# First attention of a four-stage network: four buffers for the x rows and another order of turns, loads and small operations

## The chip, the cores and the metric

The kernel runs on one core of a Trainium2 chip. The core has TensorE (PE, with its weight loads PEld), VectorE (DVE), ScalarE (ACT), GpSimd (POOL), and SyncE (SP), which here issues nearly all DMAs. The metric is the device time of one execution in microseconds (us). The kernel before took 2070.7 us, the median of 3 runs (2068.66 to 2072.9).

## The reference

The network has four stages: an attention (L0_xattn), a mixture of experts (L0_ffn), a second attention (L1_xattn) and a second mixture (L1_ffn). Only the first stage, its last batch's preparations for the second, and the first loads are touched by the change. Cut to what matters:

```python
# stage 1, four batches b; context ctx is 512x256, x is 512x512 per batch
query = einsum('bnc,dc->bnd', teacher_features, Wq) + bq      # d = 128
key = einsum('bnc,dc->bnd', teacher_features, Wk) + bk
attention = softmax(einsum('bnd,bmd->bnm', query, key), axis=-1)
x_m = einsum('bln,bmn->blm', teacher_logits, attention)       # x rows are normalised first
# stage 3 needs keys and values of the same context: k = _ln(y @ Wk + bk), v = y @ Wv + bv
# stage 2: gate = x @ Wg[e] + x @ Ga[e] @ Gb[e], and so on
```

The kernel computes stage 3's keys (with their norm over heads of 32) and values inside stage 1, because the context is on the core there, and parks them in DRAM.

## The kernel before, in words

Every product in fp32 accuracy is made of three TensorE products of high and low halves (`mm3`, lines 55 to 57); ACT makes the high half (a copy), DVE or POOL the low half (the difference). So every operand goes through ACT and then DVE before TensorE can use it. The five engines run five programs written out by hand, each in strict order; semaphores (`then_inc`, `wait_ge`) join them. No scheduler moves anything.

The first attention (`first_attention`) runs four batches b. For each batch TensorE does, in this order: four key products (`key_or_value`, 0 to 3), transposition of the normalised x rows (`x_turn`, four of them, through line 101), query and key of the next batch (`query_or_key`), transposition of the attention shares (`at_turn`), four value products, the next batch's scores (`scores`), four mixed products (`mixed`: shares times x) with transpositions of the normalised keys between them (`k_turn`).

What the names mean: `CT` is the loaded context, `CYh` and `CYl` its halves (`split_ct_act`, `split_ct_low`); `XNa` the normalised x rows (`normal`, on ACT, two buffers), `XTah` and `XTal` the halves of their transposition; `ATa` the shares, `ATTah` and `ATTal` the halves of their transposition; `KW` the raw keys, `KQ` their squares (`square`), `ksum` and `vv` the variances, `yy` their power -1/2 (POOL, `pow`); `VO` the values on their way to DRAM (two buffers); `KG`, `KH`, `KL` normalised keys and their halves; `qTa`, `kTa` the query and key; `KId` a table of picks that POOL builds in rows of `ATa` and SP stores, so that the first exponentials may only overwrite `ATa` once that store has landed (`st_ki`). `WK`, `WKd`, `WV`, `WVd` are key and value weights; of the first two the means over each head are taken off first (`head_means`, `center`). `stats` and `row_factors` make the norm of the x rows (DVE, then POOL).

In batch 3 there is no next batch; TensorE does low-rank products of the first expert's gate (g) and up (u) weights there (`lora_pe`, line 1209), DVE adds them to the loaded weights `STG` (`lora_dve`, line 1329), ACT and DVE make halves `Wg0h`, `Wg0l`.

A bank of PSUM or a buffer is reused only after its readers are through: `x_turn` n waits for `XTal` n-2 (`freed67`), `normal` k for the transposition k-2, `mixed` 2 for the update of `X` that reads bank 0 (`o_x`).

## Time and profile before

| what | us |
|---|---|
| median of 3 runs | 2070.7 |
| the profiled execution, whole | 2068.12 |
| its span, first to last instruction | 2066.3 |
| TensorE busy in the span | 1994.7 (97%) |
| stage 1 until its last transposition of keys ends | 207.15 |
| TensorE busy in those | 169.82 |
| TensorE waits in them, before the first product | 10.5 |

The profile is of one execution. An engine's time is split into instructions, and the idle time before one is put down to the instruction or DMA that released it. TensorE is near full from stage 2 on; the idle time lies in the first tenth. "PEclk" or "clock" is the TensorE clock that was granted: 1.00 is 2.4 GHz and a stretch at 1.2 GHz counts half. A product of 512 columns starts 0.23 us after the one ahead at the full clock and 0.43 us after it at the low one; as it lasts 0.39 us at the full clock, a stop also costs the overlap of some 0.2 us.

### The profile page before, as it was taken

What the parts mean: (1) busy time and instruction counts of PE and PEld (TensorE: products, weight loads), DVE (VectorE), ACT (ScalarE), POOL (GpSimd) and SP (SyncE); (2) the same over time, 40 slices, a digit from 0 to 9 for tenths busy, and PEclk for the clock granted to TensorE, in tenths of its full rate; (3) what the DMA queues carried; (4) which work ended last, traced back from release to release, by engine and by line L of the source; (5) the groups of instructions that cost most, each with busy time, mean ns of one, the idle gap of its engine ahead of it and who ended that gap; (6) DMA issues with size and microseconds to landing.
All of it is one profiled execution on the core that took longest, in us unless ns stands there. A gap on an engine that the chain in (4) does not pass through costs nothing. (4 is left out here: it accounts for less than half of the span.)

```text
span 2066.3 us, 29550 instructions
## 1 busy us (share of the span) xinstructions
PE 1994.7 (97%) x11805; PEld 1585.1 (77%) x11805; DVE 945.7 (46%) x1555; ACT 767.6 (37%) x1210; POOL 675.9 (33%) x629
## 2 busy tenths in 40 slices
PE   6888999999999999999999999999999999999997
PEld 4776687788888888888888888756666667889996
DVE  6775433222222222221221245687677664656664
ACT  5464611212212121121211222356565655247664
POOL 5444301011101111011111127446464323226674
PEclk9998999999999999999999999999999999999999
DMA  5232200103012030010100001734343330169994
GB/s 196 77 128 90 74 1 26 41 1 123 21 63 81 1 122 21 21 41 1 41 21 19 28 1 44 179 73 102 84 103 88 73 118 32 42 226 269 264 270 112
DMA packets 91336, 171.32 MB, mean 83 GB/s; under 512 B 10864, under 2 KB 35952, under 8 KB 88240
## 3 DMA queue, kind: packets, MB, share of 16 engines
q1 hardware_dynamic: 80896, 148.96, 23.5%
q0 software_dynamic: 10304, 20.47, 4.5%
q8 instruction: 94, 1.54, 0.3%
q14 instruction: 42, 0.34, 0.1%
HBM read 131.51 MB, written 54.13 MB: 90 GB/s over the span
## 5 line engine op out<-in xcount | busy, mean ns | idle before, releaser
L1570 POOL TENSOR_TENSOR ML<-MT,MH 128x512 fp32r<-128x512 f32 x128 | 164.9, 1292 | 791.2 <-ACT MH L1372 791.0
L1514 DVE SCALAR_TENSOR_TENSOR X<-PS,WT,X 128x512 f32<-128x512 f32 x128 | 96.0, 750 | 391.1 <-PE PS L57 390.6
L1372 ACT ACTIVATE MH<-MT 128x512 fp32r<-128x512 f32 x128 | 80.9, 632 | 512.1 <-DVE MT L1441 512.1
L55 PE MATMUL PS<-HH,Wg0h 128*128 128x512 f32 x512 | 200.6, 392 | 0.2 <-issue 0.2
L55 PE MATMUL PS<-Wd0h,MH 128*128 128x512 f32 x512 | 199.6, 390 | 0.1
L56 PE MATMUL PS<-HL,Wg0h 128*128 128x512 f32 x512 | 199.7, 390 | 0.0
L57 PE MATMUL PS<-HH,Wg0l 128*128 128x512 f32 x512 | 199.6, 390 | 0.0
L55 PE MATMUL PS<-HH,Wu0h 128*128 128x512 f32 x512 | 199.5, 390 | 0.0
L56 PE MATMUL PS<-HL,Wu0h 128*128 128x512 f32 x512 | 199.3, 389 | 0.0
L57 PE MATMUL PS<-HH,Wu0l 128*128 128x512 f32 x512 | 199.2, 389 | 0.0
L56 PE MATMUL PS<-Wd0l,MH 128*128 128x512 f32 x512 | 199.2, 389 | 0.0
L57 PE MATMUL PS<-Wd0h,ML 128*128 128x512 f32 x512 | 199.2, 389 | 0.0
L1441 DVE TENSOR_TENSOR MT<-PS,SG 128x512 f32<-128x512 f32 x128 | 88.4, 690 | 232.2 <-POOL ML L1570 159.8
L1979 ACT ACTIVATE PTB<-PS 128x512 f32<-128x512 f32 x256 | 138.7, 595 | 111.4 <-PE PS L1904 110.5
L2063 DVE TENSOR_REDUCE VB<-PS 128x2 f32<-128x992 f32 x232 | 148.9, 684 | 41.7 <-PE PS L1889 41.4
L1343 ACT ACTIVATE SG<-PS 128x512 f32<-128x512 f32 x128 | 76.4, 597 | 224.4 <-PE PS L57 224.4
L55 PEld LDWEIGHTS PS<-HH,Wg0h 128*128 128x128 f32 x512 | 96.4, 188 | 21.9 <-issue 2.1
L55 PEld LDWEIGHTS PS<-HH,Wu0h 128*128 128x128 f32 x512 | 96.1, 188 | 21.7 <-issue 1.5
L55 PEld LDWEIGHTS PS<-Wd0h,MH 128*128 128x128 f32 x512 | 96.1, 188 | 21.4 <-issue 1.3
L57 PEld LDWEIGHTS PS<-HH,Wg0l 128*128 128x128 f32 x512 | 96.4, 188 | 20.3
L56 PEld LDWEIGHTS PS<-HL,Wg0h 128*128 128x128 f32 x512 | 96.4, 188 | 19.8
L57 PEld LDWEIGHTS PS<-Wd0h,ML 128*128 128x128 f32 x512 | 96.1, 188 | 20.1
(481 smaller groups left out, 4300.6 us busy)
## 6 DMA issues: line engine op xcount, KB each, us to landing
RAW<-Wd SPq DMA_DIRECT2D x23, 1536.0 KB
HH<-Kd SPq DMA_DIRECT2D x48, 256.0 KB, 4.1
HL<-Qd SPq DMA_DIRECT2D x48, 256.0 KB, 6.3
STG<-in_Wg SPq DMA_DIRECT2D x8, 1024.0 KB, 5.2
STG<-in_Wu SPq DMA_DIRECT2D x8, 1024.0 KB, 5.2
STG<-in_Wd SPq DMA_DIRECT2D x8, 1024.0 KB, 5.3
X<-in_x SPq DMA_DIRECT2D x16, 256.0 KB, 8.5
Vd<-VO SPq DMA_DIRECT2D x16, 256.0 KB, 2.0
```

The source lines that it names most:

```text
L55: e.matmul(out_, a_[0], b_[0], start=start, stop=False)
L56: e.matmul(out_, a_[0], b_[1], start=False, stop=False)
L57: return e.matmul(out_, a_[1], b_[0], start=False, stop=stop)
L1343: e.activation(SG[:, f, :], PS[:, bank["g", i], :], ACT.Silu).then_inc(g_silu, 1)
L1372: e.activation(M[0][:, f, :], MT[i % 2][:, :], ACT.Copy).then_inc(m_h, 1)
L1441: e.tensor_tensor(MT[i % 2][:, :], PS[:, bank["u", i], :], SG[:, f, :], ALU.mult).then_inc(u_mul, 1)
L1514: e.scalar_tensor_tensor(X[:, k, :], PS[:, bank["d", 4 * n + q], :], WT[:, k, x:x + 1], X[:, k, :], ALU.mult, ALU.add).then_inc(d_x, 1)
L1570: e.tensor_tensor(M[1][:, f, :], MT[i % 2][:, :], M[0][:, f, :].bitcast(f32), ALU.subtract).then_inc(m_l, 1)
L1979: e.activation(PT[u % 2][:, 2 * pr:2 * pr + 2, :], PS[:, p % 2, :].rearrange("p (h q) -> p h q", h=2), ACT.Exp, scale=SCALE).then_inc(t_ex ...
L2063: e.tensor_reduce(MX[s % 2][:, q:q + 2, h, t], PS[:, SBANK:SBANK + 2, lo:hi], axis=X_, op=ALU.max).then_inc(s_max, 1)
```

## The change

Eight things change, all in the first attention (and in what it does ahead for stage 2):

1. The x rows get four buffers: the two `VO` buffers join `XN`. All four `normal` of batches 1 to 3 are done at the end of the batch before; in batch 0 the last two come later. `value` waits for the transposition of the row that lay in its `VO`.
2. TensorE's order: x rows 0 and 1, then query and key of the next batch together, then x rows 2 and 3; the first value product stands ahead of the first transposition of shares. Query and key wait for the first piece of `CYl` only. ACT and DVE follow that order; `square` 3 and `variance` 1 move behind x row 1.
3. DVE does values 0 and 1 earlier (before and after the first two `ATTal`), and the next batch's first maxima and exponentials after the second `ATTal`.
4. The variance is finished, and the power taken, for 16 heads at a time, four times a batch, rather than once for 64.
5. SP loads the context first, then the query and key weights; `g` and `temp` follow later.
6. In `picks_pool` the selects work on two columns and are then copied out to 512.
7. At the start the low half of `WKd` moves from POOL to DVE, the order of centring changes.
8. In batch 3 the low-rank products and their sums go in halves, with the low half of the gate weight behind the norm of the keys.

```diff
     def picks_pool(e, rows):
-        e.memset(rows, 1.0).then_inc(made_ki, 1)
+        e.memset(rows[:, :, 0:512:511], 1.0).then_inc(made_ki, 1)
...
+        for lo, hi, at in ((1, 496, 0), (496, 511, 511)):
+            e.tensor_copy(rows[:, :, lo:hi], rows[:, :, at:at + 1].to_broadcast([16, 4, hi - lo])).then_inc(made_ki, 1)
...
+        XN += VO
...
         def sp(e):
-            e.dma_start(bqk[:, 0:2], a["bqk0"]).then_inc(ld_qk, 16)
+            load_ct(e, 0)
...
         def query_or_key(e, b, j):
-            e.wait_ge(ct_l, 3 * b + 3)
+            e.wait_ge(ct_l, 3 * b + 1)
...
             if b == 0 and v == 0 and n == 0:
-                e.wait_ge(k_sub, 3)
+                e.wait_ge(k_sub, 2)
...
-                for j in range(2):
-                    x_turn(e, b, 2 * j)
-                    x_turn(e, b, 2 * j + 1)
-                    if more:
-                        query_or_key(e, b + 1, j)
+                x_turn(e, b, 0)
+                x_turn(e, b, 1)
+                if more:
+                    query_or_key(e, b + 1, 0)
+                    query_or_key(e, b + 1, 1)
+                else:
+                    two_front["lora_pe"](e, "g", 0)
+                x_turn(e, b, 2)
+                x_turn(e, b, 3)
                 if b == 3:
-                    two_front["lora_pe"](e, "g", 0)
                     two_front["lora_pe"](e, "g", 1)
                 for j in range(4):
+                    key_or_value(e, b, 4 + j)
                     if j % 2 == 0:
                         at_turn(e, b, j)
                         at_turn(e, b, j + 1)
-                    key_or_value(e, b, 4 + j)
...
         def normal(e, k):
-            if k >= 2:
-                e.wait_ge(xt_mm, k - 1)
-            e.activation(XN[k % 2][:, :], X[:, k, :], ACT.Identity, bias=nmr[:, k:k + 1],
+            if k >= 4:
+                e.wait_ge(xt_mm, k - 3)
+                if k % 4 >= 2:
+                    e.wait_ge(st_v[k % 2], 32 * (k // 4))
+            e.activation(XN[k % 4][:, :], X[:, k, :], ACT.Identity, bias=nmr[:, k:k + 1],
...
+                    if more and n == 1:
+                        query_or_key_high(e, b + 1, 0)
+                        query_or_key_high(e, b + 1, 1)
+                    if n == 1:
+                        square(e, b, 3)
+                    if b == 0 and n == 1:
+                        normal(e, 2)
+                        normal(e, 3)
+                        shares(e, 0, 0)
+                        shares(e, 0, 1)
...
-                    normal(e, 4 * b + 4)
-                    normal(e, 4 * b + 5)
+                    for k in range(4 * b + 4, 4 * b + 8):
+                        normal(e, k)
...
+            at = slice(16 * n, 16 * n + 16)
+            e.tensor_reduce(ksum[:, at], heads(KQ[n % 2][:, :]), axis=X_, op=ALU.add).then_inc(k_var, 1)
+            e.wait_ge(k_var, 2 * i + 1)
+            e.tensor_scalar(vv[:, at], ksum[:, at], 1.0 / 32, 1e-6, ALU.mult, ALU.add).then_inc(k_var, 1)
...
-            center(e, chain, slice(0, 2))
+            query_or_key_low(e, 0, 0)
+            center(e, chain, slice(0, 1))
+            query_or_key_low(e, 0, 1)
+            big_low(e, 0, k_sub)
             maxima(e, 0, 0)
-            big_low(e, 0, k_sub)
+            center(e, chain, slice(1, 2))
             e.wait_ge(ld_bias, 64)
             head_means(e, chain, slice(2, 4))
             center(e, chain, slice(2, 4))
+            big_low(e, 1, big_l)
...
+                    if b == 3 and n % 2:
+                        two_front["add"](e, "g", n // 2)
...
                 if b == 3:
-                    two_front["low"](e, "g")
-                    two_front["add"](e, "u")
-                e.wait_ge(k_pow, b + 1)
+                    two_front["add"](e, "u", 1)
+                e.wait_ge(k_pow, 4 * b + 4)
...
+                if b == 3:
+                    two_front["low"](e, "g")
...
-                e.wait_ge(k_var, 5 * b + 5)
-                e.tensor_tensor(yy[:, :], vv[:, :], mhalf[:, :], ALU.pow).then_inc(k_pow, 1)
+                for n in range(4):
+                    at = slice(16 * n, 16 * n + 16)
+                    e.wait_ge(k_var, 2 * (4 * b + n) + 2)
+                    e.tensor_tensor(yy[:, at], vv[:, at], mhalf[:, at], ALU.pow).then_inc(k_pow, 1)
...
+        def lora_half(e, n, half):
+            for c in (2 * half, 2 * half + 1):
+                lora_sum(e, 4 * n + c)
```

TensorE in batch 1, as a difference: rows of the next batch's query (`wqT`) and key (`wkT`), of x transposed from `XNa` or `VO`, of shares `ATa` and of values (`WV1`).

```order
 L57 MATMUL PS<-CY0h,wqTl 128x512
-L101 MATMUL PS<-ident,XNa 128x128 x8
 L55 MATMUL PS<-CY0h,wkTh 128x512
 L56 MATMUL PS<-CY0l,wkTh 128x512
@@ -207,5 +206,5 @@
 L56 MATMUL PS<-CY0l,wkTh 128x512
 L57 MATMUL PS<-CY0h,wkTl 128x512
-L101 MATMUL PS<-ident,ATa 128x128 x8
+L101 MATMUL PS<-ident,VO 128x128 x8
 L55 MATMUL PS<-WV1h,CY1h 128x512
 L56 MATMUL PS<-WV1l,CY1h 128x512
```

The second pair of x transpositions moved from between query and key to behind them, and now reads the two `VO`.

ACT in batch 0, behind the first two normalised x rows, before:

```order
L428 ACTIVATE KQ0<-KW 128x512
L428 ACTIVATE KQ1<-KW 128x512
L490 ACTIVATE XTah<-PS 128x4x128
L421 ACTIVATE XNa0<-X,nmr,rstd0 128x512
L490 ACTIVATE XTah<-PS 128x4x128
L421 ACTIVATE XNa1<-X,nmr,rstd0 128x512
L401 ACTIVATE qTah<-PS,bqk 128x512
L490 ACTIVATE XTah<-PS 128x4x128 x2
L401 ACTIVATE kTah<-PS,bqk 128x512
```

The same place on ACT now:

```order
L443 ACTIVATE KQ0<-KW 128x512
L504 ACTIVATE XTah<-PS 128x4x128 x2
L414 ACTIVATE qTah<-PS,bqk 128x512
L414 ACTIVATE kTah<-PS,bqk 128x512
L443 ACTIVATE KQ1<-KW 128x512
L436 ACTIVATE VO0<-X,nmr,rstd0 128x512
L436 ACTIVATE VO1<-X,nmr,rstd0 128x512
L448 ACTIVATE ATa0<-ATa0,sma 128x512 x4
L504 ACTIVATE XTah<-PS 128x4x128 x2
```

The last two normalised rows (now in `VO`) moved behind the high halves of query and key, and the four shares (`ATa`, which stood ahead of the first normalised row) stand behind them.

DVE in batch 3, from the last row means to the update of `X`, before:

```order
L1433 BN_AGGR mv<-st 128x2 x4
L1321 TENSOR_TENSOR Wg0l<-STG00,Wg0h 128x2048
L1329 TENSOR_TENSOR STG01<-PS,STG01 128x512 x4
L674 TENSOR_TENSOR tt_<-yy 128x64
L676 TENSOR_TENSOR tt_<-tt_,vv 128x64
L678 TENSOR_SCALAR tt_<-tt_ 128x64
L680 TENSOR_TENSOR yy<-yy,tt_ 128x64
L683 TENSOR_TENSOR KW<-KW,yy 128x512 x4
L692 SCALAR_TENSOR_TENSOR X<-PS,TG,X 128x512 x2
```

The same place on DVE now:

```order
L1473 BN_AGGR mv<-st 128x2 x4
L1365 TENSOR_TENSOR STG01<-PS,STG01 128x512 x2
L704 TENSOR_TENSOR tt_<-yy 128x64
L706 TENSOR_TENSOR tt_<-tt_,vv 128x64
L708 TENSOR_SCALAR tt_<-tt_ 128x64
L710 TENSOR_TENSOR yy<-yy,tt_ 128x64
L713 TENSOR_TENSOR KW<-KW,yy 128x512 x4
L1357 TENSOR_TENSOR Wg0l<-STG00,Wg0h 128x2048
L727 SCALAR_TENSOR_TENSOR X<-PS,TG,X 128x512 x2
```

The low half `Wg0l` moved from ahead of the sums of the up weight to between the norm of the keys and the update of `X`.

## Rows read from the trace of the kernel before

**Rows 1.** The page: the span and TensorE's busy time, share and instructions.
```profile
span 2066.3 us, 29550 instructions
...
PE 1994.7 (97%) x11805; PEld 1585.1 (77%) x11805; DVE 945.7 (46%) x1555; ACT 767.6 (37%) x1210; POOL 675.9 (33%) x629
```
**Rows 2.** Stretches: length; busy PE, PEld, DVE, ACT, POOL; TensorE clock; DMA share, GB/s.
```profile
0.00:37.01 37.01, 16.61 (x55) 12.46 (x55) 26.67 (x53) 17.73 (x32) 15.67 (x29) 0.93 0.70 252
37.01:77.26 40.25, 38.65 (x181) 31.62 (x182) 25.10 (x53) 23.94 (x46) 24.61 (x18) 0.94 0.26 93
77.26:119.77 42.51, 37.84 (x181) 30.77 (x180) 30.91 (x69) 23.84 (x46) 19.34 (x20) 0.96 0.15 56
119.77:161.47 41.70, 36.90 (x181) 29.50 (x180) 31.32 (x66) 22.53 (x43) 21.67 (x22) 1.00 0.42 140
161.47:207.15 45.68, 39.82 (x144) 26.43 (x143) 27.36 (x48) 16.67 (x26) 15.95 (x9) 0.81 0.26 92
```
**Rows 3.** What TensorE waited for, 0 to 207.1: total, times, longest, in us.
```profile
PE PS L101 <- DVE XTal L646: 9.0, 6, 2.7
PE PS L55 <- DVE WK1l L555: 3.3, 1, 3.3
PE PS L55 <- DVE VO L603: 3.3, 4, 0.9
PE PS L1209 <- DVE STG L1329: 2.4, 1, 2.4
PE PS L55 <- DVE X L692: 2.2, 3, 0.9
```
**Rows 4.** Instructions in order of time, batch 0: start, length, and idle before.
```profile
3.18 0.94 SPq L231 DMA_DIRECT2D CTa<-in_ctxT  x2
...
20.65 0.69 ACT L415 ACTIVATE ATa<-PS,mxa 128x512 f32<-128x512 f32 x1 [1.35 <-DMA KId<-ATa]
...
29.67 2.46 DVE L547 BATCH_NORM_STATS2 st<-X 128x6 f32<-128x512 f32 x4
...
33.70 2.55 ACT L433 ACTIVATE ATa<-ATa,sma 128x512 f32<-128x512 f32 x4
...
35.37 0.24 POOL L718 TENSOR_SCALAR nmr<-nmr 128x4 f32<-128x4 f32 x1
...
37.01 1.97 PE L101 MATMUL PS<-ident,XNa 128*128 128x128 f32 x8 [4.98 <-ACT XNa L421]
```
**Rows 5.** The same in batch 1, in the order the prediction uses them.
```profile
73.58 1.51 ACT L421 ACTIVATE XNa<-X,nmr,rstd 128x512 f32<-128x512 f32 x2
...
78.99 0.63 ACT L428 ACTIVATE KQ<-KW 128x512 f32<-128x512 f32 x1 [1.51 <-DVE ksum L596]
...
82.14 0.63 PE L101 MATMUL PS<-ident,XNa 128*128 128x128 f32 x4 [2.46 <-DVE XTal L646]
...
101.54 2.50 DVE L683 TENSOR_TENSOR KW<-KW,yy 128x512 f32<-128x512 f32 x4
```
**Rows 6.** The same in batch 2: DVE's low context, and POOL beside it.
```profile
118.19 2.71 DVE L527 TENSOR_TENSOR CY1l<-CTa,CY1h 128x1024 fp32r<-128x1024 f32 x3 [1.61 <-ACT CY1h L395]
```
**Rows 7.** The same in batch 3: low-rank products, and the gate weight's low half.
```profile
167.21 7.33 PE L1209 MATMUL PS<-LB,LA 64*128 64x512 f32 x8
...
190.55 2.26 DVE L1321 TENSOR_TENSOR Wg0l<-STG,Wg0h 128x2048 fp32r<-128x2048 f32 x1
...
193.56 1.95 PE L1209 MATMUL PS<-LB,LA 64*128 64x512 f32 x4 [2.40 <-DVE STG L1329]
```
**Rows 8.** Small DVE operations beside POOL ones, at the start and in stage 3.
```profile
23.13 2.37 POOL L555 TENSOR_TENSOR WKd1l<-KW,WKd1h 128x1024 fp32r<-128x1024 f32 x1 [12.37 <-ACT WKd1h L455]
...
23.28 2.25 DVE L567 TENSOR_SCALAR means<-means 128x32 f32<-128x32 f32 x1
...
1240.11 2.90 POOL L1002 TENSOR_TENSOR yy<-vv,mhalf 128x16 f32<-128x16 f32 x1
...
1242.27 0.17 DVE L982 TENSOR_SCALAR gs<-gs 128x16 f32<-128x16 f32 x1
```

More of the change, by code:

```diff
@@ L370, in pe @@
                         at_turn(e, b, j + 1)
-                    key_or_value(e, b, 4 + j)
-                    if more and j % 2:
+                    elif more:
                         scores(e, b + 1, j // 2)
@@ L483, in act @@
                     split_ct_act(e, b + 1)
-                for n in range(0 if b else 2, 4):
+                for n in range(0 if b else 2, 3):
                     square(e, b, n)
@@ L501, in act @@
                     e.activation(ATT[0][:, c, :], PS[:, 6 + c % 2, :], ACT.Copy).then_inc(at_h, 1)
-                if more:
-                    exponentials(e, b + 1, 0)
-                    exponentials(e, b + 1, 1)
-                    shares(e, b + 1, 0)
+                    if more and c == 1:
+                        exponentials(e, b + 1, 0)
                 if b == 3:
@@ L509, in act @@
                     two_front["high"](e, "u")
+                if more:
+                    exponentials(e, b + 1, 1)
                 keys_high(e, b, 0)
                 if more:
+                    shares(e, b + 1, 0)
                     shares(e, b + 1, 1)
@@ L629, in dve @@
                 stats(e, 0, k)
+            temperature(e)
             for n in range(4):
@@ L642, in dve @@
                 key(e, 4 * b + 3)
-                variance(e, 4 * b + 1)
                 for n in range(4):
@@ L647, in dve @@
                                     XT[0][:, :, n * P:(n + 1) * P].bitcast(f32), ALU.subtract).then_inc(xt_l, 1)
-                    if more and n % 2:
-                        query_or_key_low(e, b + 1, n // 2)
+                    if n == 1:
+                        variance(e, 4 * b + 1)
+                    if more and n == 1:
+                        query_or_key_low(e, b + 1, 0)
+                        query_or_key_low(e, b + 1, 1)
+                    if b == 3 and n % 2:
+                        two_front["add"](e, "g", n // 2)
                 variance(e, 4 * b + 2)
                 variance(e, 4 * b + 3)
-                e.wait_ge(k_var, 5 * b + 4)
-                e.tensor_scalar(vv[:, :], ksum[:, :], 1.0 / 32, 1e-6, ALU.mult, ALU.add).then_inc(k_var, 1)
-                if b == 3:
-                    two_front["add"](e, "g")
                 for c in range(4):
+                    if c % 2 == 0:
+                        value(e, 4 * b + c)
+                    if b == 3 and c == 2:
+                        two_front["add"](e, "u", 0)
                     e.wait_ge(at_h, 4 * b + c + 1)
@@ L660, in dve @@
                     if c % 2:
-                        value(e, 4 * b + c // 2)
-                        if c == 3 and more:
+                        value(e, 4 * b + c)
+                        if c == 1 and more:
                             maxima(e, b + 1, 0)
@@ L665, in dve @@
                             row_stats(e, b - 1, (0, 1))
-                value(e, 4 * b + 2)
-                value(e, 4 * b + 3)
                 if b:
@@ L684, in dve @@
                                     ALU.mult).then_inc(k_norm, 1)
-                if more:
-                    maxima(e, b + 1, 1)
+                if b == 3:
+                    two_front["low"](e, "g")
                 for n in range(4):
                     k = 4 * b + n
-                    if more:
-                        recip(e, k + 4)
+                    if more and n == 0:
+                        maxima(e, b + 1, 1)
+                        for m in range(2):
+                            recip(e, 4 * b + 4 + m)
+                    if more and n == 2:
+                        for m in range(2, 4):
+                            recip(e, 4 * b + 4 + m)
                     e.wait_ge(o_mm, k + 1)
@@ L1552, in first_mixture @@
             lora_pe=lambda e, which, half: lora_pe(e, 0, which, (half,)), high=lambda e, which: weight_h(e, 0, which),
-            add=lambda e, which: lora_dve(e, 0, which), low=lambda e, which: weight_l(e, 0, which),
+            add=lambda e, which, half: lora_half(e, nth(0, which), half), low=lambda e, which: weight_l(e, 0, which),
             row=row, router_high=router_high, stat=row_stat, mean=row_mean, factors=factors)
```

58 lines of the change are left out of this document (27 added, 31 removed).

## The prediction

> **What bounds the kernel now.** The page comes first: TensorE is busy for 97% of the span [rows 1]. Then the table of stretches, cut at each batch's first transposition of x [rows 2]: TensorE works 16.6, 38.7, 37.8, 36.9 and 39.8 us in 207.15 us, so 37.3 us of the whole kernel's idle 72 lie here. No other engine is full (DVE 141 us of 207), so the stage is bound by chains between engines, not by an engine. The clock column tells a second loss: a mean of 0.81 over the last 45.68 us means that 2 x 0.19 x 45.68 = 17 us went by at 1.2 GHz, in which half of the work is lost; batches 1 and 2 have 0.96 and 1.00. The list of waits names the chains [rows 3]: 9.0 us for the low half of transposed x (XTal, a long and a short one in each of batches 1 to 3, so 3.0 a batch), 3.3 for the first key weight, 3.3 for a value leaving its bank (0.8 a batch), 2.4 for the low-rank sums, 2.2 for the update of X (0.7 in each of batches 0 to 2); the first normalised x row adds 4.98 [rows 4]. From stage 2 on TensorE has hardly a gap, so I carry what stage 1 gains to the end one for one.
>
> I go by batch, each from its first x transposition. Where no row has a length, an operation of 512 columns counts 0.6 to 0.7 us on DVE or ACT (four statistics took 2.46, a square 0.63) [rows 4, 5].
>
> **Start and batch 0: about -0.5.** The context was issued at 3.18 [rows 4], behind five transfers; now it is first. The weights of query and key come behind it and are needed too, so the first product gains between 0 and 2.4 us; I take 1.5. Statistics of x begin at 29.67 on DVE [rows 4]. Ahead of them DVE loses a stall of 2.05 (a scale of 32 columns took 2.25 beside POOL's WKd1l, which goes) [rows 8] and gets that WKd1l itself, 1.13 by half of a 2048-column difference [rows 7]. So they begin at 29.67 - 1.5 - 2.05 + 1.13 = 27.25. POOL's factors were through at 35.61, 5.94 later, but the normalised row waited for four shares until 36.15 and reached TensorE at 37.01 [rows 4]. The shares now stand behind, so TensorE starts at 27.25 + 5.94 + 0.86 = 34.05: 3.0 us of head start. The wait for WK1l (3.3) lies ahead of this point and is no further gain; the five or so microseconds that the keys gain there end in a longer wait for x. The first exponentials waited for the picks' store until 20.65 [rows 4]; as many bytes stand ahead of it as before, so small selects are worth 0 there (a microsecond either way at most).
>
> Then batch 0 gives it back. Rows 2 and 3 of x are normalised only behind both high halves of query and key and a square: 0.69 + 0.63 + 0.75 on ACT after TensorE's last key product, a wait of 2.1. Behind them on ACT stand the fourth row, four shares (2.55) and XTah, then XTal on DVE: 4.6 us against 2.5 of TensorE work, a wait of 1.9 before the shares are transposed. Every stop also costs the overlap of two products, 0.2. That is 4.4, against one stop of 1.0 for a value before: +3.4. The stop for X before the third mixed product (0.9) goes, since DVE has done its maxima by then. Sum -3.0 + 3.4 - 0.9 = -0.5. Ends: -4 if the new waits were hidden, +3 if no head start came.
>
> **Batch 1: -3.1.** Before: 3.0 for XTal (its long wait is the 2.46 at 82.14) [rows 5], 0.8 for a value, 0.7 for X [rows 3], four overlaps, and some 0.8 lost to the low clock (0.04 x 2 x 42.5 = 3.4 us low, half of it idle) [rows 2]: 6.1. After: ACT does four normalisations where it did two (1.51), so the context's halves come 1.5 later, and CYl ends about 1.0 after TensorE's first x transposition. Behind it on DVE stand key 2, variance 0 and its scale, then ACT's third square, which waits for that variance already (1.51 at 78.99) [rows 5], then XTah and XTal: five steps of 0.6, so XTal is there 4.1 after. TensorE now has two transpositions and both query and key (0.8 + 2.9) before it asks: a wait of 0.4, then 0.2. New: XTah 2 stands behind two high halves and a square, so the transposition of shares waits 0.8 and 0.15. The value's wait goes: values 0 and 1 leave earlier, and what value now waits for, a row's transposition, is long over. X comes later against TensorE: from the last value product DVE has that value, the row statistics (2.8), the Newton step (1.0), the norm (2.50) [rows 5], maxima and X, 9.4 us against 7.9 of scores, two mixed products and two transpositions: 1.5. Sum after 3.05. The power is never late: its first pieces run while DVE is elsewhere. Ends: -6 and 0.
>
> **Batch 2: -0.9.** Before: the same 3.0, 0.8, 0.7 and overlaps, no low clock [rows 2, 3]: 5.3. After: as batch 1, but the low context took 2.71 here [rows 6], since its small pieces stood beside POOL's KL; later by 1.5, it meets that work again, 1.4 more: 4.4. Ends: -4 and +1.
>
> **Batch 3: -6.9.** Before: 3.0 for XTal, 0.8 for a value, 2.40 for the sums [rows 3, 7] and overlaps, 6.9; the low clock: eight passes of low-rank products took 7.33 at 0.92 each, where four took 1.95 later, 0.49 each: 3.4 lost [rows 7]; the transpositions and first value products around them lose 2.6 by the same ratio, and the rest of the 17 us low I put at 1.7. Together 14.6. After: TensorE has a low-rank half (2.0) between the x transpositions, which hides most of XTal: 0.2 and 0.2; the second half waits 0.9 for the sums, which are now behind XTal and a variance. The u products no longer wait. But the gate's low half (2.26) [rows 7] now stands between the norm and X: 1.45 before the key transpositions and 2.0 behind them. 4.75 in waits. From the first transposition to the first value there are then some 7 us with transpositions, low-rank passes and waits only, which before went low; I let the clock fall for one stretch, 2.3, and give 0.6 for the chance of another at the X wait. 7.7. Difference -6.9; ends -11 (no low clock, X hidden) and 0.
>
> The Trainium skill speaks against this part ("TensorE: Matmul & The Clock Gate", section "PE-mode transpose"): transpositions do not count as TensorE being busy for the clock. This case's rows agree as far as the low-rank passes of 167.21 and what stands round them stayed at 1.2 GHz. By that rule the 2.3 stays; without it batch 3 would give -9.2.
>
> **Powers in quarters.** DVE gets four scales of 16 heads a batch for one of 64, 0.5 us more, beside POOL's powers. A scale of 32 columns was held to the end of a POOL difference (23.13 + 2.37 = 25.50; 23.28 + 2.25 = 25.53), but one of 16 beside a power of 2.90 took 0.17 [rows 8]. So 0.5 in all over the batches' slack: 0. The Trainium skill ("SBUF — State Buffer", section "SBUF: two separate sides") has the ports that VectorE and GpSimd share as an exclusive lock, held for a whole instruction by who comes first. The first pair of rows agrees, the second does not; by the rule the time is that of the port rival.
>
> **Sum.** -0.5 - 3.1 - 0.9 - 6.9 = -11.4 on the profiled execution's 2068.1 (span 2066.3 and 1.8 around it) is 2056.7. That execution lies 2.6 below the median of 2070.7, so I forecast 2059, with 2053 to 2065 for this case alone.
>
> **Rivals.**
> - *The new waits are hidden.* TensorE's waits of 4.4, 3.05, 4.4 and 4.75 vanish too, because ACT and DVE run ahead further than I count. For: neither is over 76% busy in any stretch [rows 2]. Against: each wait is a count of operations in strict order. 2059 - 16.6 = 2042. Chance 0.14.
> - *The four normalisations hold up batches 1 and 2.* The context's halves, 1.5 later, push key 2, the squares and XTal by more than TensorE's extra 1.45 of key products covers, and X's wait grows: the 4.0 of these batches is lost. For: DVE is busy 31 of 42 us there and strictly ordered. 2063. Chance 0.15.
> - *The port.* Each scale behind a running power waits for its end, up to 2.9; the third and fourth of a batch come close enough to lose some 2.3 on DVE, half of which reaches TensorE: 4 x 1.2, so 2064. Against: the row of 0.17. Chance 0.08.
> - *The clock turns it round.* What happened round the low-rank products of batch 3 happens in all four batches, since x transpositions, waits and share transpositions now stand nearer together: 6.0 lost in each (3.4 + 2.6), of which 2.3 is already counted. 2059 + 4 x 6.0 - 2.3 = 2081; with two batches low so the gain is all but gone, from the third it is slower. For: three of the four batches went low before. Against: batch 2 had its long wait and kept 1.00 [rows 2]. Chance 0.06.
>
> The forecast keeps 0.57. Faster by over 0.2% is under 2066.6 (about what can be told from no change): nearly all of the forecast, the first rival, most of the second and third, 0.82. Within 0.2%: 0.12, from the upper ends of the second and third. Slower: 0.06, the clock. The range for 8 in 10 runs from 2046, in the first rival, to 2067, above the second and third.
>
> **What would show it.** The first product near 9.0; the first x transposition near 34, then two waits near 2 in batch 0 on a normalised row in VO and on XTal; in batches 1 and 2 XTal waits under 1.5 and X waits of 1.5; no wait for VO or the low-rank u sums; in batch 3 X late behind Wg0l, and a clock over 0.9. I am wrong if the first value of a batch starts later against its first x transposition than before, if a scale of 16 takes over 1 us, or if stage 2 takes up a gap that stage 1 gave.

## The result, and the profile after

The changed kernel took 2058.25 us (median of 5 runs, 2050.63 to 2061.13) against 2072.90 for the kernel before in the same comparison: a ratio of 0.9925, with a 95% interval from 0.990 to 0.995. Faster was right, and 2059 was forecast. The profiled execution took 2061.13 us, the longest of the five, as before's (2068.12) was shorter than all five of its runs; so the sum is tested on the stretches of the traces rather than on these two totals.

The page after: span, TensorE, and the granted clock by fortieths of the span.

```profile
span 2059.1 us, 29588 instructions
...
PE 1993.1 (97%) x11805; PEld 1586.0 (77%) x11805; DVE 946.1 (46%) x1568; ACT 767.6 (37%) x1210; POOL 672.1 (33%) x642
...
PEclk9998999999999999999999999999999999999998
```

The same stretches as in [rows 2], cut at the first transposition of x of each batch (last transposition of keys, first product with the low-rank rows of Wd as the last two cuts; columns as there):

```profile
0.00:33.62 33.62, 17.07 (x55) 12.45 (x55) 23.18 (x54) 14.87 (x28) 9.25 (x30) 0.95 0.77 277
33.62:75.64 42.02, 39.44 (x181) 32.11 (x181) 26.24 (x55) 27.36 (x51) 26.01 (x21) 0.92 0.25 89
75.64:114.77 39.13, 36.58 (x181) 29.47 (x180) 30.73 (x70) 23.45 (x46) 20.94 (x24) 1.00 0.16 61
114.77:154.99 40.22, 36.59 (x181) 29.47 (x180) 32.86 (x72) 23.10 (x45) 22.67 (x25) 1.00 0.41 145
154.99:191.47 36.48, 33.18 (x140) 22.83 (x139) 27.56 (x50) 14.74 (x23) 17.42 (x15) 0.95 0.35 113
191.47:213.63 22.16, 18.09 (x86) 14.35 (x84) 9.53 (x17) 16.34 (x27) 9.55 (x11) 0.77 0.33 112
```

TensorE's waits up to 215 us, which answer to [rows 3] (total, times, longest):

```profile
PE PS L55 <- DVE X L727: 4.6, 3, 1.9
PE PS L101 <- ACT QY L1396: 3.9, 2, 3.6
PE PS L101 <- DVE XTal L674: 3.8, 5, 1.5
PE PS L101 <- ACT XNa L436: 3.2, 1, 3.2
PE PS L101 <- ACT VO L436: 2.1, 1, 2.1
PE PS L101 <- DVE KW L713: 1.3, 1, 1.3
PE PS L1245 <- DVE STG L1365: 0.2, 1, 0.2
```

XTal fell from 9.0 to 3.8, the values' 3.3 are gone, the low-rank sums' 2.4 became 0.2; X grew from 2.2 to 4.6, and VO, KW and a long QY are new. The kernels by stretch, in us (batch 3 to its last transposition of keys, "front" from there to the first low-rank product of Wd):

| kernel | ratio to before | x starts | b 0 | b 1 | b 2 | b 3 | front | sum |
|---|---|---|---|---|---|---|---|---|
| before | 1 | 37.01 | 40.25 | 42.51 | 41.70 | 45.24 | 19.43 | 226.14 |
| changed | 0.9925 | 33.62 | 42.02 | 39.13 | 40.22 | 36.48 | 22.16 | 213.63 |
| e1 low early | 0.9900 | 34.52 | 41.76 | 39.15 | 40.24 | 32.81 | 18.30 | 206.78 |
| e2 batch 3 undone | 0.9960 | 33.85 | 42.06 | 39.11 | 40.24 | 43.65 | 18.28 | 217.19 |
| e3 batch 0 rows early | 0.9913 | 33.23 | 38.71 | 39.14 | 40.27 | 36.48 | 21.86 | 209.69 |
| e4 power whole | 0.9937 | 33.76 | 45.14 | 39.56 | 40.71 | 34.87 | 21.44 | 215.48 |
| e5 three edits | 0.9889 | 33.52 | 38.71 | 39.26 | 40.21 | 32.00 | 19.54 | 203.24 |
| e6 variance back | 0.9929 | 33.34 | 41.44 | 38.61 | 39.73 | 36.45 | 22.20 | 211.77 |
| e7 query, key apart | 0.9937 | 33.26 | 41.50 | 39.38 | 40.48 | 36.33 | 21.72 | 212.67 |
| e8 old loads | one run | 33.91 | 42.86 | 39.11 | 40.24 | 34.91 | 22.51 | 213.54 |
| e9 old selects | one run | 34.36 | 41.81 | 40.13 | 40.25 | 36.33 | 19.21 | 212.09 |
| e10 square back | 0.9950 | 33.46 | 41.09 | 41.82 | 40.81 | 37.47 | 21.70 | 216.35 |
| e11 two buffers | 0.9915 | 33.74 | 41.78 | 38.54 | 39.54 | 37.08 | 20.01 | 210.69 |
| e12 e5, context first | 0.9878 | 34.12 | 38.70 | 37.99 | 38.79 | 31.99 | 20.04 | 201.63 |

Each ratio is to runs of the kernel before in the same comparison (medians 2071.29 to 2073.83); each row of stretches is from one profile.

The changed kernel leads by 12.5 at the end of this table. What is left of the span took between 1839.8 and 1845.9 in all fourteen profiles (1840.2 before, 1845.5 after), with no pattern in the edits: that spread makes the two profiled totals only 7 apart. The medians are 14.7 apart, so the lead is not lost behind the table. A part of the spread is the clock: in the 130 us that begin 1510 us behind the end of the table it was 0.99 in five profiles (before, e5, e8, e9, e12; the rest took 1839.8 to 1844.0) and 0.97 in the other nine (1842.9 to 1845.9).

The rows also tell what a stretch is worth as a measure. In the kernels whose edits leave a stretch alone, batch 2 repeats to 0.06, and batch 1 to 0.15 but for e9. Batch 3 and the front do not: in the kernels that leave it alone, batch 3 took 36.33 to 36.48 (changed, e3, e7, e9) or 34.91 (e8), and the front, wherever Wg0l is late (see e1 below), 19.21 to 22.51.

### The profile page after: what moved, and what is told of

Its sections match the earlier page's. It is cut to its first block and busy times, and to the rows that moved or that the text cites. A ratio compares the mean times of both kernels' runs of the same rounds, so it can differ in the third digit from the quotient of the medians.

```text
span 2059.1 us, 29588 instructions
## 1 busy us (share of the span) xinstructions
PE 1993.1 (97%) x11805; PEld 1586.0 (77%) x11805; DVE 946.1 (46%) x1568; ACT 767.6 (37%) x1210; POOL 672.1 (33%) x642
## 5 line engine op out<-in xcount | busy, mean ns | idle before, releaser
L57 PEld LDWEIGHTS PS<-HH,Wu0l 128*128 128x128 f32 x512 | 96.1, 188 | 20.1
```

What stands on the lines that cost most here:

```text
L57: return e.matmul(out_, a_[1], b_[0], start=False, stop=stop)
```

## The experiments

**Where batch 3's stops and the front's come from.** In the changed kernel VectorE makes Wg0l at 180.78, between the norm of the keys and X.

```diff
                         value(e, 4 * b + c)
+                        if b == 3 and c == 1:
+                            two_front["low"](e, "g")
...
-                if b == 3:
-                    two_front["low"](e, "g")
                 for n in range(4):
                     k = 4 * b + n
```

> The changed kernel with one edit: in batch 3 the low half of the gate weight (Wg0l) is made on VectorE right behind the second value, in a gap of 2.1 us, rather than between the norm of the keys and X. Theory A: the place of Wg0l is what made batch 3 stop for X (1.86), and, since its end releases the 1 MB load of the next weight just ahead of the stores of the key halves, also what made these stores late (4.3 to 4.9 us instead of 2.1 to 2.5) and so the stop of 3.60 for row QY that stage 2's front shows. Then the X stop goes, the QY stop falls to 2.2 or less, and of the low clock behind them some goes too: about 5 us less than the changed kernel (2053, between -3 and -8). Rival B: the QY stop is ACT's and POOL's own chain of key halves, too late for a faster TensorE wherever the load stands; then only the X stop goes, the QY stop stays at 3 or grows, and the time falls by 2 or less.

Measured: 2052.90 (ratio 0.990, 0.9885 to 0.9915). First the changed kernel's rows on SP, ACT and PE (start, length, idle before):

```profile
183.09 0.39 SPq L1194 DMA_DIRECT2D STG<-in_Wd  x1
183.53 0.50 SPq L287 DMA_DIRECT2D Kd<-KH  x1
...
183.87 0.47 PE L55 MATMUL PS<-ATTah,XTah 128*128 128x512 f32 x1 [1.86 <-DVE X L727]
...
192.94 0.63 ACT L463 ACTIVATE KH<-KG 128x512 fp32r<-128x512 f32 x1 [2.95 <-DMA Kd<-KL]
...
196.54 1.09 PE L101 MATMUL PS<-ident,QY 128*128 128x128 f32 x4 [3.60 <-ACT QY L1396]
```

(`KH`, `KL` go to DRAM as `Kd`; `QY` is a normalised row of x for stage 2.) Then e1's, on SP and PE:

```profile
175.07 0.59 SPq L1194 DMA_DIRECT2D STG<-in_Wd  x1
184.10 0.33 SPq L287 DMA_DIRECT2D Kd<-KH  x1
...
181.58 1.09 PE L101 MATMUL PS<-ident,KW 128*128 128x128 f32 x8 [1.26 <-DVE KW L715]
...
192.19 0.63 PE L101 MATMUL PS<-ident,QY 128*128 128x128 f32 x4 [2.24 <-ACT QY L1396]
```

And e1's batch 3 and front as stretches (length, PE busy, clock, DMA share, GB/s):

```profile
155.67:188.48 32.81, 31.36 (x139) 1.00 0.36 127
188.48:206.78 18.30, 14.40 (x85) 1.00 0.39 132
```

The weight load is issued 0.4 us ahead of the key stores in the one and 9 us ahead in the other. The first two of these stores, with the time from issue to landing at the end of a line, in the changed kernel and under it in e1:

```profile
Kd<-KH SPq DMA_DIRECT2D x1, 256.0 KB, 6.6
Kd<-KL SPq DMA_DIRECT2D x1, 256.0 KB, 8.1
```

```profile
Kd<-KH SPq DMA_DIRECT2D x1, 256.0 KB, 3.1
Kd<-KL SPq DMA_DIRECT2D x1, 256.0 KB, 2.3
```

So the stores right behind the load were later than e1's expectation has it: its 4.3 and 4.9 are medians of four stores, of which two stood behind the load. In the changed kernel ScalarE waits 2.95 for such a store before it may write KH again, and row QY stands behind that. In the nine kernels with Wg0l late, ScalarE waited 1.03 to 4.57 for that store, and the QY stop was 2.24 (twice) to 5.18; in the five with Wg0l early (e1, e5, e12) or in its old place (before, e2) ScalarE never waited, and the stop was 2.24. Theory A is shown for the stops. Its sizes, 3.7 us in batch 3 and 3.9 in the front, hold a part that comes and goes with the clock. In e4 and e8 the stop for X is 1.86 too, but batch 3's clock is 1.00; e4's row:

```profile
159.17:194.04 34.87, 31.57 (x140) 1.00 0.32 104
```

So 2.1 of the 3.7 (34.9 against 32.81) go with the stop itself, the rest with the clock. In the front, the median is 21.72 in the nine kernels with Wg0l late and 19.43 in the other five: some 2.3 is what repeats.

**Batch 3's part undone.** TensorE's side is below; VectorE sums g behind the last variance again, and Wg0l and the sums of u stand behind the row statistics.

```diff
-                else:
-                    two_front["lora_pe"](e, "g", 0)
                 x_turn(e, b, 2)
                 x_turn(e, b, 3)
                 if b == 3:
+                    two_front["lora_pe"](e, "g", 0)
                     two_front["lora_pe"](e, "g", 1)
...
```

> The changed kernel with the eighth part undone: in batch 3 both halves of the low-rank gate products stand behind the fourth transposition of x, their sums behind the last variance, Wg0l and the sums of u behind the row statistics, and the gate weight is loaded ahead of the low-rank rows. Theory A (the prediction's): batch 3's gain is this part's, so batch 3, from its first x transposition to its last transposition of keys, goes from 36.5 back to about 43.4 (45.2 in the kernel before), with a low clock in the low-rank passes again, and stage 2's front stops for QY as before (2.2). Together +5 to +7: about 2064. Rival B: batch 3 gains because four normalised rows are ready at its start, whatever the low-rank order; then batch 3 stays under 39 and the time within 2 of the changed kernel.

Measured: 2065.09 (0.996, 0.9947 to 0.9974), batch 3 43.65. Theory A, to 0.3 in batch 3; the front is 18.28, with the QY stop at 2.24. TensorE's stops there:

```profile
157.34 1.25 PE L101 MATMUL PS<-ident,VO 128*128 128x128 f32 x8 [1.04 <-DVE XTal L673]
163.34 2.48 PE L1243 MATMUL PS<-LB,LA 64*128 64x512 f32 x4 [2.84 <-DVE STG L1363]
184.15 2.80 PE L1243 MATMUL PS<-LB,LA 64*128 64x512 f32 x4 [3.59 <-DVE STG L1363]
```

Its batch 3 and front as stretches:

```profile
155.26:198.91 43.65, 36.18 (x140) 0.88 0.28 95
198.91:217.19 18.28, 14.39 (x86) 1.00 0.39 132
```

7.5 of stops against 3.3 in the changed kernel, and a clock of 0.88 against 0.95: 10.5 us low against 3.6, half of it lost. 4.2 of stops and 3.4 of clock make up the 7.2 that this part is worth (the two overlap a little).

**Batch 0.** ScalarE's order there:

```diff
-            normal(e, 0)
-            normal(e, 1)
+            for k in range(4):
+                normal(e, k)
...
+                    if b == 0 and n == 1:
+                        shares(e, 0, 0)
+                        shares(e, 0, 1)
                     if more and n == 1:
                         query_or_key_high(e, b + 1, 0)
                         query_or_key_high(e, b + 1, 1)
...
```

> The changed kernel with another order on ScalarE in batch 0 alone: all four normalised rows before the first XTah, and the four shares ahead of the high halves of query and key. Theory A: the stops of 2.15 for the third row (in VO) and of 0.39 for XTal in batch 0, and the low clock right behind them, are nothing but that order; they go, nothing takes their place since TensorE has two transpositions and twelve query and key products meanwhile, and batch 0 goes from 42.0 to about 38.5: 2055. Rival B: the stop moves, to XTal (XTah then comes 1.5 later) or to the first scores (query and key later by 2.6): batch 0 stays over 41, and the time is that of the changed kernel within 1.

Measured: 2056.65 (0.9913, 0.990 to 0.9927). TensorE in batch 0, the changed kernel first, then e3:

```profile
41.56 1.94 PE L101 MATMUL PS<-ident,VO 128*128 128x128 f32 x8 [2.15 <-ACT VO L436]
...
45.92 1.23 PE L101 MATMUL PS<-ident,ATa 128*128 128x128 f32 x8 [0.39 <-DVE XTal L674]
```

```profile
38.78 1.03 PE L101 MATMUL PS<-ident,VO 128*128 128x128 f32 x8
...
42.26 1.22 PE L101 MATMUL PS<-ident,ATa 128*128 128x128 f32 x8 [1.06 <-DVE XTal L672]
```

Batch 0 is 38.71 as expected, though not quite by theory A: the stop for VO goes, that for XTal comes to 1.06. In the changed kernel the low clock behind the first stop (a transposition of 1.94 for 1.03) hid it; in e1, where that transposition took 1.33 behind the same stop of 2.15, it was 1.65. So of the 3.3 a part is the clock (0.92 over batch 0 in the changed kernel, 0.96 in e3 and e1): against e1, with a clock as in e3, the order is worth 3.0. The gain of 3.3 in the trace is 1.6 in the medians, inside their spread.

**Powers.**

```diff
-                for n in range(4):
-                    at = slice(16 * n, 16 * n + 16)
-                    e.wait_ge(k_var, 2 * (4 * b + n) + 2)
-                    e.tensor_tensor(yy[:, at], vv[:, at], mhalf[:, at], ALU.pow).then_inc(k_pow, 1)
+                e.wait_ge(k_var, 8 * b + 8)
+                e.tensor_tensor(yy[:, :], vv[:, :], mhalf[:, :], ALU.pow).then_inc(k_pow, 1)
...
```

> The changed kernel with the fourth part half undone: POOL takes the power of all 64 heads in one instruction per batch, behind the fourth variance, as the kernel before did; VectorE still finishes the variance in four pieces. Theory A (the prediction's): worth 0, since VectorE asks for the powers well behind; the Newton step of batch 3 still finds them, 3 us to spare. Within 1 us of the changed kernel. Rival B (the port): powers in pieces hold up VectorE's scales; then the whole power is faster by 3 or more. Rival C: the pieces are what made the norm early enough; then a wait for the power shows ahead of the Newton step and costs 2 or more.

Measured: 2060.67 (0.9937, 0.9922 to 0.9953). e4's batch 0, on POOL, DVE and PE:

```profile
49.01 10.59 POOL L762 TENSOR_TENSOR yy<-vv,mhalf 128x64 f32<-128x64 f32 x1 [8.37 <-DVE vv L620]
...
59.63 0.23 DVE L704 TENSOR_TENSOR tt_<-yy 128x64 f32<-128x64 f32 x1 [3.06 <-POOL yy L762]
...
63.19 1.09 PE L101 MATMUL PS<-ident,KW 128*128 128x128 f32 x8 [0.55 <-DVE KW L713]
65.63 0.47 PE L55 MATMUL PS<-ATTah,XTah 128*128 128x512 f32 x1 [1.35 <-DVE X L727]
```

Theory A falls, C holds in batches 0 to 2: one power of 10.6 comes 3.06 late, and TensorE stops 0.55 for KW in each, in batch 0 also for X: 3.1, 0.4 and 0.5 longer, with a clock of 0.90 in batch 0. The port falls too: in the changed kernel, a scale of 16 beside a running power took 0.18 (below).

**All three gains together.** Beside the edits of e1 and e3, the Newton step and half of the norm go ahead of the last sums of u:

```diff
-                if b == 3:
-                    two_front["add"](e, "u", 1)
                 e.wait_ge(k_pow, 4 * b + 4)
...
                 for n in range(4):
+                    if b == 3 and n == 2:
+                        two_front["add"](e, "u", 1)
                     e.tensor_tensor(heads(KW[:, n, :]), heads(KW[:, n, :]), over(yy[:, 16 * n:16 * n + 16], 32),
```

> The changed kernel with three edits: Wg0l early, as in the first experiment; batch 0's four normalised rows and shares early, as in the third; and in batch 3 the Newton step and the norm of the first two keys ahead of the last two sums of u. Theory A: each edit takes away its own stop, and the gains add: 7.7 from batch 3 on by the first trace, 3.3 in batch 0 by the third, and the stop of 1.26 for KW at the first transposition of keys in batch 3 falls under 0.3. By the traces 12, by the medians of the two runs 5.4 and 1.6 and another 1: between 2046 and 2051, I take 2049. Rival B: they share one thing (a stretch at the low clock, or stage 2's front, which starts at a fixed time), so the sum is that of the larger alone: 2053.

Measured: 2048.36 (0.9889, 0.9872 to 0.9905). The gains add in the stretches that the edits touch: batch 0 as in e3, batch 3 0.8 under e1; the KW stop is 0.46, not under 0.3. The front, at 0.91 of the clock, is 1.2 longer than in e1.

**What shortened batches 1 and 2.** Four edits, one at a time.

In e6 VectorE's variance 1 goes back ahead of XTal, from behind the second one:

```diff
                 key(e, 4 * b + 3)
+                variance(e, 4 * b + 1)
                 for n in range(4):
...
-                    if n == 1:
-                        variance(e, 4 * b + 1)
```

> The changed kernel with one edit on VectorE: the variance of key 1 goes back ahead of XTal, where the kernel before had it; TensorE's order, the buffers and ScalarE's order stay. Theory A: XTal was late because VectorE waited in that variance for ScalarE's square; with it there again XTal comes about 1 us later, and TensorE stops for XTal before the third x row 0.9 to 1.5 longer in batches 1 and 2 (0.41 and 1.49 now), and less in 3: +2 to +3, so 2061. Rival B: query and key of the next batch, now together between the x rows, cover it: no stop over 0.6 more in any batch, and the time within 1 of the changed kernel.

Measured: 2057.31 (0.9929). Theory B: the stop before the third row grew by 0.3 in both batches, and that of 0.76 before the shares went. A half microsecond a batch better, not worse.

In e7 key goes behind x rows 2 and 3 in batches 1 and 2, on TensorE as shown, and likewise on ACT and DVE:

```diff
                     query_or_key(e, b + 1, 0)
-                    query_or_key(e, b + 1, 1)
+                    if b == 0:
+                        query_or_key(e, b + 1, 1)
...
+                if more and b:
+                    query_or_key(e, b + 1, 1)
...
```

> The changed kernel with query and key apart again in batches 1 and 2: query behind x rows 0 and 1, key behind rows 2 and 3, on all three engines; the four buffers, variance 1 behind XTal and the early values stay. Theory A: half of the cover for XTal is gone, so TensorE stops 1.45 longer before the third x row (1.9 and 2.9 in batches 1 and 2), and the 0.76 before the transposition of shares goes, since XTal has key's time there: +0.7 a batch, and +1.4 in all: 2060. Rival B: this is where the gain of these batches comes from, so both lose their 3.4 and 1.5: 2063. Rival C: the order is worth nothing, only buffers and variance are: within 0.5.

Measured: 2057.98 (0.9937). The stops are 1.76 and 2.86 as theory A had them, the one before the shares gone, but each batch is only 0.25 longer: nearest to C.

In e10, beside e6's edit, square 3 goes back ahead of XTah on ACT, from behind the second one:

```diff
-                for n in range(0 if b else 2, 3):
+                for n in range(0 if b else 2, 4):
                     square(e, b, n)
...
-                    if n == 1:
-                        square(e, b, 3)
```

> The changed kernel with square 3 on ScalarE back ahead of the first XTah, and so variance 1 on VectorE back ahead of XTal (which alone cost 0.3 a stop and gained 0.76 elsewhere). Theory A: the long stop for XTal before was this chain, square 3 waiting for variance 1 with all of XTah behind it: XTal then comes some 1.5 to 2 later, TensorE stops 1.5 longer before the third x row in batches 1 and 2 and shows a stop in batch 3, in sum +3 to +4: 2061. Rival B: XTal waits for the context's halves and for key 2 on VectorE in any case, so the stop grows by 0.5 or less and the time stays within 1 of the changed kernel.

Measured: 2062.04 (0.995, 0.9931 to 0.9968): theory A for the stops. ScalarE and TensorE in e10's batch 1, and the stop of batch 2:

```profile
77.79 0.63 ACT L443 ACTIVATE KQ<-KW 128x512 f32<-128x512 f32 x1 [1.51 <-DVE ksum L616]
79.19 0.63 ACT L443 ACTIVATE KQ<-KW 128x512 f32<-128x512 f32 x1 [0.76 <-DVE ksum L616]
79.72 1.06 ACT L504 ACTIVATE XTah<-PS 128x512 fp32r<-128x512 f32 x2
...
81.08 1.96 PE L101 MATMUL PS<-ident,VO 128*128 128x128 f32 x8 [1.91 <-DVE XTal L673]
...
123.05 1.26 PE L101 MATMUL PS<-ident,VO 128*128 128x128 f32 x8 [2.88 <-DVE XTal L673]
```

Two squares, each waiting for a variance on VectorE, stand ahead of XTah; batches 1 to 3 are 2.7, 0.6 and 1.0 longer. Of the 2.7 not all is the edit's. The clock has a part (0.96 over the batch, the transposition of 1.96). And in e9, whose edit lies at the start alone, batch 1 is 1.0 longer too: in both, ScalarE had waited for a key half's store at the end of batch 0, which it does not in the changed kernel. e10, then e9:

```profile
68.79 0.63 ACT L463 ACTIVATE KH<-KG 128x512 fp32r<-128x512 f32 x1 [1.04 <-DMA Kd<-KL]
```

```profile
70.46 0.63 ACT L460 ACTIVATE KH<-KG 128x512 fp32r<-128x512 f32 x1 [1.08 <-DMA Kd<-KL]
```

That leaves 1.7 for the edit and the clock in batch 1, and 0.6 in batch 2.

In e11 two buffers serve from batch 1 on, and the last two rows stand behind the first and second XTah:

```diff
-                    for k in range(4 * b + 4, 4 * b + 8):
+                    for k in range(4 * b + 4, 4 * b + 6):
                         normal(e, k)
...
+                    if b and n < 2:
+                        normal(e, 4 * b + n + 2)
...
```

> The changed kernel with only two buffers for the x rows from batch 1 on: the last two rows of a batch are normalised behind the first and second XTah, as before, the values wait for no transposition, and all orders else stay. Theory A: the four buffers by themselves are worth little, since ScalarE gives back at the end of a batch (1.51, so the context's halves come 1.5 earlier) what it pays behind XTah: within 1.5 of the changed kernel, the stop for XTal before the third row near 0 and a stop for the row itself, or for XTal before the shares, of 0.8 to 1.5 in its place. Rival B: the four buffers carry batches 1 and 2, and without them 3.4 and 1.5 are lost: 2063.

Measured: 2056.17 (0.9915, 0.9894 to 0.9937). Theory A: batches 1 and 2 are 0.6 and 0.7 shorter with two buffers, batch 3 0.6 longer. The four buffers carry none of the gain of batches 1 to 3.

**The head start.** e8 has g, biases and weights of query and key ahead of the context on SP again; e9 has POOL's wide fills and selects again, without the copies:

```diff
         def sp(e):
+            consts_sp(e)
+            e.dma_start(bqk[:, 0:2], a["bqk0"]).then_inc(ld_qk, 16)
-            load_ct(e, 0)
             for j, name in enumerate(("wqT0", "wkT0")):
...
+            load_ct(e, 0)
             load_big(e, 0)
```

> The changed kernel with the first six loads in the order of the kernel before (g, query and key biases and weights, then the context); the small selects and the rest stay. Read from the trace alone, by the start of the first product (8.97 in the changed kernel, 10.54 before) and of the first x transposition (33.62). Theory A (the prediction's): the context ahead of the weights is what brought the first product 1.5 earlier, so it comes at 10.5 again, and x about 1 to 1.5 later. Rival B: it was the selects, which no longer slow down VectorE's first differences (2.08 beside a select before, 0.43 now); then the first product stays under 9.5.

```diff
-        e.memset(rows[:, :, 0:512:511], 1.0).then_inc(made_ki, 1)
+        e.memset(rows, 1.0).then_inc(made_ki, 1)
...
-        for lo, hi, at in ((1, 496, 0), (496, 511, 511)):
-            e.tensor_copy(rows[:, :, lo:hi], rows[:, :, at:at + 1].to_broadcast([16, 4, hi - lo])).then_inc(made_ki, 1)
```

> The changed kernel with the sixth part undone: POOL fills and selects all 512 columns of the picks again; the context stays first. Read from the trace, by the first product (8.97 in the changed kernel, 9.34 with the old order of loads, 10.54 before). After the run with the old loads, theory A: the selects held up VectorE's first differences (2.08 beside one before, 0.43 and 0.45 with the small ones), and they are worth most of the 1.57: the first product comes at 10.0 or later, and the first exponentials, which wait for the picks' store, at 20 or later (19.27). Rival B (the prediction's): the small selects are worth 0, the first product stays under 9.5.

One profile each (2057.50 and 2057.78 us): the first product came at 9.34 in e8, at 10.10 in e9. In the other profiles with the changed start it came between 8.73 and 9.36, so e8's cannot be told from them: the order of loads is worth some 0.4, if anything. e9's POOL and VectorE, and under it the changed kernel's VectorE:

```profile
4.63 5.44 POOL L143 TENSOR_SCALAR_AFFINE_SELECT ATa<-ATa 16x1984 f32<-16x1984 f32 x4
...
6.70 2.08 DVE L632 TENSOR_TENSOR wkTl<-XNa,wkTh 128x256 fp32r<-128x256 f32 x1
```

```profile
6.69 0.43 DVE L635 TENSOR_TENSOR wkTl<-XNa,wkTh 128x256 fp32r<-128x256 f32 x1
```

The wide selects hold up a small difference by 1.65, and with it the context's low half: the selects gave the first product 1.1 of its 1.57. x itself came at 33.91 in e8 and 34.36 in e9, the first exponentials at 20.01 and 20.29; in e1, whose start is that of the changed kernel, they came at 34.52 and 21.09. So what the selects give the first product is not shown to reach x.

**One step more.** On e5, the next context's high halves go ahead of x rows 2 and 3:

```diff
                 if b in (1, 2):
                     split_ct_act(e, b + 1)
+                if b:
+                    normal(e, 4 * b + 2)
+                    normal(e, 4 * b + 3)
...
-                    for k in range(4 * b + 4, 4 * b + 8):
+                    for k in range(4 * b + 4, 4 * b + 6):
                         normal(e, k)
```

> The best kernel so far (three edits, 2048.4) with one more: at the turn of batches, ScalarE makes the high halves of the next context before rows 2 and 3 of x rather than behind them. Theory A: the context's low half, on VectorE, is 1.5 late because ScalarE does four rows first (VectorE waits 2.6 for the halves), and key 2, the variance and XTal stand behind it; with the halves earlier the stops for XTal of 0.53 and 1.50 in batches 1 and 2 go, and nothing comes for the rows, which TensorE asks for 4 us later: -1.5 to -2.5, about 2046.5. Rival B: XTal is held by ScalarE's third square and not by the context, so the stops stay: within 0.7 of 2048.4.

Measured: 2047.53 (0.9878, 0.986 to 0.9895). Both stops for XTal before the third row are gone, and batches 1 and 2 are 1.3 and 1.4 shorter than in e5: theory A in the trace. The medians differ by 0.8 only, which their spread does not tell from 0.

## Why the prediction was right, and where it was not

By its own steps, predicted and measured, each against before:

| step | predicted | measured |
|---|---|---|
| start (first x transposition) | -3.0 | -3.4 |
| batch 0 from there | +2.5 | +1.8 |
| batch 1 | -3.1 | -3.4 |
| batch 2 | -0.9 | -1.5 |
| batch 3 | -6.9 | -8.8 |
| stage 2's front | 0 | +2.7 |
| sum | -11.4 | -12.5 |

The sum is nearer than its terms, which is in part luck: batch 3 gave 1.9 more than forecast and four other steps 2.0 more between them, and the front, which the sum had at 0, took 2.7 back. That the median came within 1 of 2059 says less still, as the kernel before ran at 2072.9 this time instead of 2070.7.

**Start.** Right in sum: x at 33.62, forecast 34.05. The statistics began at 26.70 (forecast 27.25), and the scale of 32 columns took 0.18 where it had 2.25, as counted. One term had the wrong cause: 1.5 was put on the context's place among the loads and 0 on the selects; for the first product e8 and e9 show it the other way round.

**Batch 0.** The new waits came where they were put: 2.15 for the third row (2.1), and 0.39 for XTal (1.9) because the clock had fallen to 1.2 GHz behind the first; at the higher clock of e1 it is 1.65. The first is ScalarE's order alone: e3 takes it away; XTal's stays there at 1.06. One of the prediction's own signs of being wrong came here: the first value starts 9.53 after the batch's first x transposition, against 8.03 before. In the other batches it comes earlier (5.21 against 10.23 in batch 1).

**Batches 1 and 2.** The stops came at 0.41, 0.76 and 1.35 in batch 1 (forecast 0.4 and 0.2, 0.8, 1.5), and 1.49 for the first in batch 2. The mechanism was half told. I gave the gain to the covering order of TensorE and the early values; by e10 up to 2.3 of the 4.9 in both, a part of it clock, are the square and the variance that no longer stand ahead of XTah, by e7 TensorE's order is worth 0.25 a batch, and by e11 the four buffers nothing. What the early values give was not undone by itself: the value's stops of 0.79 and 0.80 are gone, and the stops for X grew from 0.87 and 0.57 to 1.35. That the context comes late behind four normalisations was right, as e12 shows.

**Batch 3.** The stops were 0.19, 1.25 and 1.86 (forecast 0.2 and 0.2, 0.9, 1.45, 2.0). The mis-sized term is the clock: before, 0.19 x 2 x 45.24 = 17.2 us were low, half of it lost (8.6); after, 0.05 x 2 x 36.48 = 3.6, so 1.8 lost. That is 6.8 gained where 7.7 less 2.9 was counted. It did not fall at the transpositions and low-rank passes either (1.00 from 155 to 175), but behind the stop for X. In e1 passes and transpositions stand as they did, the X stop is gone, and the clock is 1.00 throughout. The stop alone does not settle it, though: in e4 and e8 it is 1.86 as well, and the clock of batch 3 is 1.00. The rule of the Trainium skill on transpositions ("TensorE: Matmul & The Clock Gate", section "PE-mode transpose"), by which the prediction kept a loss of 2.3 round the low-rank passes, is not borne out at them; it is not refuted either, since no run has the stops without transpositions.

**Front.** The step that failed is "I carry what stage 1 gains to the end one for one". What was counted as a wait inside batch 3, Wg0l behind the norm, had a second price outside it: it releases a 1 MB load onto the stores of the key halves. The QY stop grew from 2.24 to 3.60, and TensorE went on at 0.77 of its clock against 0.91 before: 2.7 in all, of which by the medians of all kernels some 2.3 goes with the place of Wg0l. That is the prediction's other sign of being wrong, a gap that stage 2 takes up. Behind the front nothing is shown to take up the gain.

**Powers.** The cost of 0 was right, and so was the reason given under batch 1, that the first pieces run while VectorE is elsewhere: taken whole, the power comes 3.06 late (e4). What falls is e4's theory A, by which VectorE asks late enough for a whole one.

**Rivals.** Hidden waits: no, they are there. Four normalisations: they do hold up the context, but cost 1.3 and 1.4 (e12), 2.7 of the 4.0. The port: beside a power, the changed kernel's VectorE is not held up, while beside a difference of 512 columns it is:

```profile
47.26 5.76 POOL L764 TENSOR_TENSOR yy<-vv,mhalf 128x16 f32<-128x16 f32 x2 [1.01 <-DVE vv L620]
...
47.80 0.18 DVE L620 TENSOR_SCALAR vv<-ksum 128x16 f32<-128x16 f32 x1
...
153.24 2.54 POOL L774 TENSOR_TENSOR KL<-KG,KH 128x512 fp32r<-128x512 f32 x2
...
154.71 1.10 DVE L620 TENSOR_SCALAR vv<-ksum 128x16 f32<-128x16 f32 x1
```

The clock: batch 0 has 0.92, batches 1 and 2 1.00; it turned nothing round.

Open: what beside the clock makes the rest of the span vary by 6 us between profiles; why the same stop brings the clock down in one profile and not in another; and the share of the four buffers in batch 0, where they were not undone.

## What to carry to other kernels

When an operation is moved, ask what its end releases, not only what it delays: a weight load that a difference sets free can land on the stores that another engine waits for. Undo a many-part change part by part and read the stretches of the traces, but first see from kernels that leave a stretch alone how well it repeats: here batch 2 showed 0.3 us, batch 3 and the front not 1.5. Differences of 2 us were lost in the medians. The part in the title (four buffers) was worth nothing from batch 1 on, and the best version (0.9878) came from four moves that the traces' new stops pointed to. A stop can be hidden by a low clock, so a stop that is taken away may show another behind it.

## What the runs showed of the hardware

A small VectorE operation beside POOL took 2.08 us beside a select of 16x1984 (0.43 without) and 1.10 beside a difference of 128x512, but 0.17 to 0.18 beside a power that ran for 2.9 us: it depends on what POOL does. Four stores of 256 KB that were issued 0.4 to 3.3 us behind a 1 MB load landed after 6.3 to 8.1 us; in e1, with the load 9 us ahead, the same four took 2.3 to 3.1. A stop of 1.86 us in batch 3 went with a granted clock of 0.95 over the batch in seven kernels and of 1.00 in two.
